# Biases of a linear attention carried by a constant feature of the normalised input, and the query feature map read from PSUM

## The chip, the cores and the metric

One core of one Trainium2 chip. The metric is the device time in microseconds (us) of one execution of the program. The engines are named as in the profile: PE is TensorE (matmul), PEld its weight load, DVE is VectorE, ACT is ScalarE, POOL is GpSimd, SP is SyncE, and a trailing q (SPq) is an engine's queue.

## The reference, cut to what matters

Four residual layers run on an input of 4 batches x 2048 tokens x 256 features. Only the first, a linear attention, is touched by the change:

```python
x = inputs                                    # (4, 2048, 256)
z = (x - mean(x)) / sqrt(var(x) + 1e-5)       # layer norm over the 256 features, no gain
q = elu(z @ Wq + bq) + 1;  k = elu(z @ Wk + bk) + 1;  v = z @ Wv + bv
kv = einsum('bkhd,bkhm->bhdm', k, v)          # 16 heads of 16
out = einsum('bqhd,bhdm->bqhm', q, kv) / max(einsum('bqhd,bkhd->bqh', q, k), 1e-6)
x = x + out @ Wo + bo
```

Then follow a feed-forward layer, a second attention that only reaches 16 tokens of each batch, and the feed-forward layer again. A normalised row has mean zero, so its 256 features sum to zero, and feature 255 is minus the sum of the others.

## The kernel before, in words

The 8192 tokens are cut into 16 groups (n = 0 to 15) of 512 tokens, four groups to a batch; a group is four tiles of 128 tokens. **Pass 1** (to about 190 us) computes for each group the normalised input, keys and queries, and adds k^T z up over a batch in PSUM; **pass 2** computes the attention output and the rest. Every engine has its own instruction stream, in an order written out by hand, and waits on semaphores. The change touches pass 1 and the loads ahead of it.

For each group in pass 1 PE runs, in this order: `k_product` (L1078: for each tile one bf16 matmul of `ones_row` by `bias3`, which puts bk + 1 into PSUM, then six fp32r matmuls of 256 columns, hi and lo halves of input and weights) into PB; at a batch's first group `g_transposes` of the batch before; `q_product` (L1091: 12 fp32r matmuls of 512 columns) into PA, with `kv_product` of the batch before in its middle at a batch's first group; `t1` (L1055: 8 transposes of the next group's normalised input into PT); `g_product` (L1105: 8 fp32 matmuls, 16 in the trace, of 257 columns: 256 features and a column of ones whose product is the sum of k) into PG.

ACT: normalises the next group (`ln1`, L516, four instructions at L513), takes exp of k - 1 (L541), then for each half of the queries exp (L548) and relu (L549), both with bq as bias, then copies the transposed input as `xt_hi` (`t1`, L524). DVE: `k_tok` = max(min(exp, 1), PSUM) (L722), statistics of the group after the next (L668, L671), at a batch's first group `batch_kv` (L740), `xt_lo` (L681), then the query step (L732), min(exp, 1) + relu, with both inputs in SBUF. Ahead of a batch's first group it copies PG to `g_sb` (`copy_g`, L734). PE's `q_product` waits on `q_relu` of the group before.

POOL turns statistics into scale and shift (`rstd`, L419, L424 to L430), and adds `bo` to x (`add_bo`, L441). POOL waits for `w2_loaded` (all seven start-up loads of L327 to L330) between its group 0 and its group 1:

```python
            ln1(0)
            pool.wait_ge(w2_loaded, 16 * 7)
            with pool.Fori(1, NG) as n:
                ln1(n)
                add_bo(n - 1)
```

The loads are issued by SP in the order x of group 0, Wq, Wk (L320), bk to three rows (L321), bq to a column (L323), Wr (L324), x of groups 1 to 3 (L326), then Wv, Wo, Ws1, Ws2, and bv, bo, ob, each spread to 128 rows (L330), then x of the groups from 4 on (L336). ACT waits for Wq and Wk (L527), splits both (L529), and only then normalises group 0. DVE computes the statistics of group 0, the lo halves (L689), the three-part bias (L693 to L700), the squares of Wr (L704) and `xt_lo` of group 0.

Of the kernel before, what the change touches and what calls it, by code (L numbers as in the profile page):

```python
# [13 lines left out]
P = 128  # L14
# [30 lines left out]
def hybrid_kernel(nc, x_in, Wq, bq, Wk, bk, Wv, bv, Wo, bo, qw, qb, kw, vw, vb, ow, ob,  # L45
# [11 lines left out]

    with ExitStack() as ctx:
# [53 lines left out]
        xn = [part(T * (D + 1)).rearrange("p (t d) -> p t d", t=T) for _ in range(2)]  # L112
# [7 lines left out]
        bias_rows = part(D)  # L120
        bpart = part(D).bitcast(BF16).rearrange("p (k n) -> p k n", k=2)
        used[0] = setup_start + 2 * C * GT
        wv, wo_raw = [part(C * D).rearrange("p (c n) -> p c n", c=C) for _ in range(2)]
        bv_rows, bo_rows = part(D), part(D)
        kv_tmp = part(C * P).rearrange("p (c n) -> p c n", c=C)
        g_sb = part(C * (D + 1)).rearrange("p (c n) -> p c n", c=C)
# [42 lines left out]
        def chunked(ap):  # L169
# [32 lines left out]
        w_loaded = sem("w_loaded")  # L202
        w2_loaded = sem("w2_loaded")
        wr_loaded = sem("wr_loaded")
        bias_loaded, bq_loaded = sem("bias_loaded"), sem("bq_loaded")
# [4 lines left out]
        bias_ready = sem("bias_ready")  # L210
# [106 lines left out]
        def _(sp):  # L317
            sp.dma_start(x_all[:, 0:T, :], x_dram[0]).then_inc(x_loaded[0], 16)
            for dst, w in ((wq_raw, Wq), (wk_raw, Wk)):
                sp.dma_start(dst, rows(w)).then_inc(w_loaded, 16)  # L320
            sp.dma_start(bias_rows[0:3, :], row(bk).to_broadcast([3, D])).then_inc(bias_loaded, 16)  # L321
            with nc.allow_non_contiguous_dma(reason="a short bias vector, features on partitions"):
                sp.dma_start(bq_col[:, :], bq.rearrange("(c p) -> p c", p=P)).then_inc(bq_loaded, 16)  # L323
# [74 lines left out]
        def _(pool):  # L398
# [47 lines left out]
            pool.wait_ge(w2_loaded, 16 * 7)  # L446
# [208 lines left out]
        def _(dve):  # L655
# [35 lines left out]
            dve.wait_ge(bias_loaded, 16)  # L691
            dve.wait_ge(consts, 5)
            link(nc.vector.tensor_scalar(bias_rows[0:3, :], bias_rows[0:3, :], 1.0, None, ALU.add))  # L693
            link(nc.vector.tensor_copy(bpart[0:3, 0, :], bias_rows[0:3, :]))
            link(nc.vector.tensor_tensor(bias_rows[0:3, :], bias_rows[0:3, :], bpart[0:3, 0, :], ALU.subtract))
            link(nc.vector.tensor_copy(bpart[0:3, 1, :], bias_rows[0:3, :]))
            link(nc.vector.tensor_tensor(bias_rows[0:3, :], bias_rows[0:3, :], bpart[0:3, 1, :], ALU.subtract))
            link(nc.vector.tensor_scalar(bias_rows[0:3, :], bias_rows[0:3, :], ident[0:3, 2:3], None, ALU.mult))
# [749 lines left out]
```

## Time and profile before

| | us |
|---|---|
| runs of the kernel before (three) | 505.45, 504.20, 504.93 |
| median | 504.93 |
| span of the profiled execution | 503.0 |
| PE / DVE / ACT / POOL busy | 454.9 / 332.7 / 271.8 / 191.4 |
| DMA moved in the profiled execution | 20.55 MB |

The span runs from the first to the last instruction of the profiled execution; the device time of that execution is not listed by itself. The median of the three runs lies 1.9 us above the span, which is what starting and ending the program adds around it. Pass 1 takes the first 190 us of the span, pass 2 the rest.

### The profile page before, as it was taken

The numbers are of one execution on the slowest core, as the hardware profiler recorded it, in microseconds if no ns is written. First come the engines' busy times: TensorE is split into PE (matmuls) and PEld (weight loads), VectorE is DVE, ScalarE is ACT, GpSimd is POOL, SyncE is SP. The second block draws the span as 40 slices with busy tenths as digits, with TensorE's granted clock in tenths as the row PEclk, the third lists the DMA queues.
The fourth block names the chain that finished last, engine by engine and source line by source line (L and its number), as shares of the span: only waits on it lengthen the run. The fifth ranks groups of instructions, "written<-read, shape, count | busy, mean of one in ns | idle before, by whom it ended". The sixth has DMA issues, their size and how long they took to land.

```text
span 503.0 us, 8738 instructions
## 1 busy us (share of the span) xinstructions
PE 454.9 (90%) x2737; PEld 369.5 (73%) x2737; DVE 332.7 (66%) x791; ACT 271.8 (54%) x465; POOL 191.4 (38%) x270
## 2 busy tenths in 40 slices
PE   1899999999999998779999899899999999996763
PEld 1888888888888887568787687576778776783441
DVE  4467766775775626365777867787876977786462
ACT  3466656665665552436566446455565465755330
POOL 2344333343433600433545436464442653334300
PEclk9999999999999999789999999999999999999895
DMA  8312111111000002000111011011101110111110
GB/s 265 122 53 76 42 43 42 44 55 43 27 1 1 1 15 70 1 1 2 61 43 51 2 44 44 1 45 43 43 3 44 44 42 1 42 42 44 41 45 7
DMA packets 22732, 20.55 MB, mean 41 GB/s; under 512 B 3155, under 2 KB 22678, under 8 KB 22678
## 3 DMA queue, kind: packets, MB, share of 16 engines
q1 hardware_dynamic: 22678, 19.92, 12.3%
q8 instruction: 23, 0.38, 0.3%
q14 instruction: 31, 0.25, 0.2%
HBM read 11.40 MB, written 8.45 MB: 39 GB/s over the span
## 4 chain that ended last, share of the span: by engine, by line
PE 61%; DVE 15%; issue 8%; ACT 6%; POOL 4%; SPq 2%; DMA 1%; DVEq 1%; POOLq 0%; ACTq 0%
PE PG L1110 8%; PE PA L1191 6%; PE PA L1211 4%; PE PG L1196 4%; PE PT L1183 3%; ACT scratch L513 3%; PE PB L1196 3%; DVE ln_bn L668 3%; PE PA L1102 3%; PE PA L1100 3%; PE PA L1101 3%; PE PB L1086 2%; PE PB L1088 2%; PE PB L1087 2%; PE PT L1061 2%
## 5 line engine op out<-in xcount | busy, mean ns | idle before, releaser
L513 ACT ACTIVATE scratch<-x_all,ln_shift,ln_rstd 128x256 f32<-128x256 f32 (+1 forms) x192 | 99.6, 589 | 69.1 <-POOL ln_shift L430 36.7
L424 POOL TENSOR_SCALAR ln_rstd<-ln_mv 128x4 f32<-128x4 f32 x48 | 10.8, 226 | 219.4 <-DVE ln_mv L671 210.0
L668 DVE BATCH_NORM_STATS2 ln_bn<-x_all 128x6 f32<-128x256 f32 (+1 forms) x192 | 67.2, 413 | 5.0 <-DMA x_all<-n_L_attn_a_inputs_q_dram 3.3
L1191 PE MATMUL PA<-scratch,ws 128*128 128x512 f32 x128 | 61.6, 604 | 1.5 <-ACT scratch L613 1.2
L1110 PE MATMUL PG<-scratch 128*128 128x257 f32 x256 | 58.5, 381 | 0.8 <-DVE scratch L722 0.8
L437 POOL TENSOR_TENSOR x_all<-x_all,ob_rows 128x1024 f32<-128x1024 f32 x16 | 37.9, 2369 | 40.3 <-ACT scratch L513 40.3
L1110 PEld LDWEIGHTS PG<-scratch 128*128 128x128 f32 x256 | 47.4, 190 | 7.7 <-issue 1.0
L426 POOL TENSOR_TENSOR ln_rstd<-ln_rstd,minus_half 128x4 f32<-128x4 f32 x48 | 49.8, 1038 | 4.0
L1183 PE MATMUL PT<-ident,scratch 128*128 128x128 f32 x256 | 36.6, 289 | 10.3 <-ACT scratch L513 9.2
L722 DVE SCALAR_TENSOR_TENSOR scratch<-scratch,PB 128x1024 f32<-128x1024 f32 x16 | 19.5, 1221 | 39.1 <-ACT scratch L541 39.1
L732 DVE SCALAR_TENSOR_TENSOR q_all<-scratch,q_all 128x1024 f32<-128x1024 f32 (+1 forms) x16 | 43.5, 2719 | 2.5 <-ACT q_all L549 2.5
L1086 PE MATMUL PB<-wk_hi,xt_hi 128*128 128x256 f32 x128 | 42.4, 331 | 0.0
L1183 PEld LDWEIGHTS PT<-ident,scratch 128*128 128x128 f32 x256 | 29.4, 147 | 16.1 <-ACT scratch L513 11.6
L437 POOL TENSOR_TENSOR x_all<-x_all,scratch 128x1024 f32 (+1 forms) x16 | 38.5, 2406 | 0.6 <-ACT scratch L513 0.6
L1191 PEld LDWEIGHTS PA<-scratch,ws 128*128 128x128 f32 x128 | 23.5, 195 | 18.6 <-issue 17.0
L1088 PE MATMUL PB<-wk_hi,xt_lo 128*128 128x256 f32 x128 | 36.8, 288 | 0.0
L1087 PE MATMUL PB<-wk_lo,xt_hi 128*128 128x256 f32 x128 | 36.7, 287 | 0.0
L681 DVE TENSOR_TENSOR xt_lo<-PT,xt_hi 128x512 fp32r<-128x512 f32 x32 | 20.7, 686 | 22.8 <-ACT xt_hi L524 22.7
L1248 PE MATMUL PB<-wo_hi,o_hi 128*128 128x256 f32 x128 | 34.0, 299 | 1.0 <-ACT o_hi L599 0.8
L852 DVE TENSOR_TENSOR x_all<-PB,x_all 128x1024 f32<-128x1024 f32 (+1 forms) x16 | 19.5, 1220 | 22.8 <-PE PB L1254 21.0
L548 ACT ACTIVATE scratch<-PA,bq_col 128x512 f32<-128x512 f32 x32 | 22.0, 688 | 22.4 <-DVE scratch L722 19.2
L594 ACT ACTIVATE scratch<-PT 128x512 f32<-128x512 f32 x32 | 17.6, 595 | 29.0 <-PE PT L1183 29.0
(194 smaller groups left out, 1029.0 us busy)
## 6 DMA issues: line engine op xcount, KB each, us to landing
x_all<-n_L_attn_a_inputs_q_dram SPq DMA_DIRECT2D x16, 512.0 KB, 3.6
out_dram<-scratch SPq DMA_DIRECT2D x16, 512.0 KB, 2.8
scratch<-in_L_attn_a_Wq_dram SPq DMA_DIRECT2D x1, 256.0 KB, 3.7
scratch<-in_L_attn_a_Wk_dram SPq DMA_DIRECT2D x1, 256.0 KB, 5.5
scratch<-in_L_attn_a_Wv_dram SPq DMA_DIRECT2D x1, 256.0 KB, 6.7
scratch<-in_L_attn_a_Wo_dram SPq DMA_DIRECT2D x1, 256.0 KB, 5.3
ws<-in_L_ffn_Ws_dram SPq DMA_DIRECT2D x2, 128.0 KB, 5.2
b_weights<-in_L_attn_b_qw_dram SPq DMA_DIRECT2D x1, 256.0 KB, 2.7
```

Of the source, the lines that this page charges most:

```text
L426: nc.gpsimd.tensor_tensor(ln_rstd[:, slot, :], ln_rstd[:, slot, :], minus_half[:, 0:T], ALU.pow).then_inc(powed, 1)
L437: nc.gpsimd.tensor_tensor(x_group(n), x_group(n), rows_[:, :].rearrange("p (o d) -> p o d", o=1).to_broadcast([P, T, D]), ALU.add).then_in ...
L513: nc.scalar.activation(dst[:, t:t + 1, 0:D], x_tile(n, t), ACT.Identity, scale=ln_rstd[:, slot, t:t + 1], bias=ln_shift[:, slot, t:t + 1]) ...
L668: nc.vector.bn_stats(ln_bn[:, slot, t:t + 1, :], x_tile(n, t)).then_inc(bn, 1)
L732: nc.vector.scalar_tensor_tensor(q, exp_q, 1.0, q, ALU.min, ALU.add).then_inc(q_done, 1)
L1086: mm(dst, hi, wk_hi[:, c, :], start=False, stop=False)
L1087: mm(dst, hi, wk_lo[:, c, :], start=False, stop=False)
L1088: last = mm(dst, lo, wk_hi[:, c, :], start=False, stop=(c == C - 1))
L1110: last = mm(PG[:, c, 0:D + 1], k_tok[:, t, c * P:(c + 1) * P], xn[g % 2][:, t, :], start=(g == 0 and t == 0), stop=(g == G - 1 and t == T ...
L1183: last = nc.tensor.transpose(dst[:, c, t * P:(t + 1) * P], src[:, t, c * P:(c + 1) * P], ident[:, :])
L1191: last = mm(dst, ws1[:, c, :], xt[:, c, :], start=(c == 0), stop=(c == C - 1))
L1196: last = mm(four(pair)[:, t, :], h[:, t * P:(t + 1) * P], ws2[:, :], start=True, stop=True)
```

## The change

Feature 255 of the normalised input is no longer computed: POOL sets that column of both buffers to 1 once, and ACT writes features 0 to 254. The weights are loaded with rows 0 to 254 in place and the bias as row 255; DVE then subtracts the old last row from the rows 0 to 254 and, for Wk and Wq, adds 1 to the bias row. So the matmuls give k + bk + 1 and q + bq + 1 with no bias matmul. The sum of k is now column 255 of `g_product`, so its 257th column goes. For the queries ACT takes exp(q - 1) in one instruction of 1024 columns and DVE computes max(min(exp, 1), PSUM) as for the keys, and PE waits for that DVE step. The loads of Wq move from SP's queue to ACT's.

```diff
+    def load_with_bias(eng, dst, last_row, w, b, loaded):
+        eng.dma_start(dst[:, 0, :], w[0:P, :]).then_inc(loaded, 16)
+        eng.dma_start(dst[0:P - 1, 1, :], w[P:D - 1, :]).then_inc(loaded, 16)
+        eng.dma_start(dst[P - 1:P, 1, :], row(b)).then_inc(loaded, 16)
+        eng.dma_start(last_row, w[D - 1:D, :].to_broadcast([P, D])).then_inc(loaded, 16)
...
 SP
             sp.dma_start(x_all[:, 0:T, :], x_dram[0]).then_inc(x_loaded[0], 16)
-            for dst, w in ((wq_raw, Wq), (wk_raw, Wk)):
-                sp.dma_start(dst, rows(w)).then_inc(w_loaded, 16)
-            sp.dma_start(bias_rows[0:3, :], row(bk).to_broadcast([3, D])).then_inc(bias_loaded, 16)
-                sp.dma_start(bq_col[:, :], bq.rearrange("(c p) -> p c", p=P)).then_inc(bq_loaded, 16)
+            load_with_bias(sp, wk_raw, wk_last, Wk, bk, w_loaded)
             sp.dma_start(wr[:, :, :], rows(Wr)).then_inc(wr_loaded, 16)
             for g in range(1, G):
                 sp.dma_start(x_all[:, g * T:(g + 1) * T, :], x_dram[g]).then_inc(x_loaded[g], 16)
-            for dst, w in ((wv, rows(Wv)), (wo_raw, rows(Wo)),
-                           (ws1[:, :, :], rows(Ws1)), (ws2[:, :], Ws2), (bv_rows[:, :], row(bv).to_broadcast([P, D])),
+            load_with_bias(sp, wv, wv_last, Wv, bv, w2_loaded)
+            for dst, w in ((wo_raw, rows(Wo)), (ws1[:, :, :], rows(Ws1)), (ws2[:, :], Ws2),
                            (bo_rows[:, :], ...), (ob_rows[:, :], ...)):
                 sp.dma_start(dst, w).then_inc(w2_loaded, 16)
 POOL
-            nc.gpsimd.memset(ones_row[:, :], 1.0).then_inc(consts, 1)
-                nc.gpsimd.memset(xn[i][:, :, D:D + 1], 1.0).then_inc(consts, 1)
+                nc.gpsimd.memset(xn[i][:, :, D - 1:D], 1.0).then_inc(consts, 1)
...
-            pool.wait_ge(w2_loaded, 16 * 7)
+            pool.wait_ge(w2_loaded, 16 * 9)
 ACT
-            act.wait_ge(w_loaded, 32)
-            for hi, raw in ((wq_hi, wq_raw), (wk_hi, wk_raw)):
-                nc.scalar.activation(hi[:, :, :], raw, ACT.Copy).then_inc(w_split, 1)
+            load_with_bias(act, wq_raw, wq_last, Wq, bq, wq_loaded)
+            act.wait_ge(wk_row, 3)
+            nc.scalar.activation(wk_hi[:, :, :], wk_raw, ACT.Copy).then_inc(w_split, 1)
             ln1(0, 0)
+            act.wait_ge(wq_row, 3)
+            nc.scalar.activation(wq_hi[:, :, :], wq_raw, ACT.Copy).then_inc(w_split, 1)
...
-                    for c in range(C):
-                        ge_apart(act, "act", q_mm, C * n + c + 1)
-                        nc.scalar.activation(exp_q[:, c, :], PA[:, c, :], ACT.Exp, bias=bq_col[:, c:c + 1]).then_inc(q_exp, 1)
-                        nc.scalar.activation(q_all[:, bass.ds(n * C + c, 1), :], PA[:, c:c + 1, :], ACT.Relu,
-                                             bias=bq_col[:, c:c + 1]).then_inc(q_relu, 1)
+                    ge_apart(act, "act", q_mm, C * (n + 1))
+                    nc.scalar.activation(exp_q, PA[:, :, :], ACT.Exp, bias=minus_one[:, 0:1]).then_inc(q_exp, 1)
 DVE
+            def take_last_row(w, last_row, done, one):
+                nc.vector.tensor_tensor(w[:, 0, :], w[:, 0, :], last_row, ALU.subtract).then_inc(done, 1)
+                nc.vector.scalar_tensor_tensor(w[:, 1, :], last_row, but_last[:, 0:1], w[:, 1, :], ALU.mult, ALU.add).then_inc(done, 1)
+                if one:
+                    dve.wait_ge(done, 2)
+                    nc.vector.tensor_scalar(w[:, 1, :], w[:, 1, :], ident[:, P - 1:P], None, ALU.add).then_inc(done, 1)
             ln1(0, 0, 0)
+            dve.wait_ge(w_loaded, 16 * 4)
+            take_last_row(wk_raw, wk_last, wk_row, True)
+            dve.wait_ge(wq_loaded, 16 * 4)
+            take_last_row(wq_raw, wq_last, wq_row, True)
...
-            (L691 to L701: the eight instructions of the three-part bias)
...
-                    ge_apart(dve, "dve", q_relu, C * (n + 1))
-                    q = q_all[:, bass.ds(n * C, C), :]
-                    nc.vector.scalar_tensor_tensor(q, exp_q, 1.0, q, ALU.min, ALU.add).then_inc(q_done, 1)
+                    ge_apart(dve, "dve", q_exp, n + 1)
+                    nc.vector.scalar_tensor_tensor(q_all[:, bass.ds(n * C, C), :], exp_q, 1.0, PA[:, :, :],
+                                                   ALU.min, ALU.max).then_inc(q_done, 1)
...
                 for c in range(C):
-                    nc.vector.scalar_tensor_tensor(kv_tmp[:, c, :], bv_rows[...], g_sb[:, c, D:D + 1], PG[:, c, D:D + P], ...)
...
             pass1(0, False)
+            dve.wait_ge(w2_loaded, 16 * 9)
+            take_last_row(wv, wv_last, wv_row, False)
 PE
-                    mm(dst, ones_row[:, :], bias3[:, :], start=True, stop=False)
...
-                ge(pe, q_relu, C * n)
+                ge(pe, q_done, n)
...
-                        last = mm(PG[:, c, 0:D + 1], k_tok[:, t, c * P:(c + 1) * P], xn[g % 2][:, t, :],
+                        last = mm(PG[:, c, 0:D], k_tok[:, t, c * P:(c + 1) * P], xn[g % 2][:, t, :],
...
+                pe.wait_ge(wv_row, 2)          (in kv_product)
```

## Rows read from the trace of the kernel before

**Rows 1.** Stretch: length, busy us of PE, PEld, DVE, ACT, POOL; clock, DMA share, GB/s.

```profile
105.00:147.00 42.00, 41.92 (x256) 36.73 (x255) 28.10 (x56) 25.88 (x44) 14.58 (x21) 1.00 0.08 25
```

**Rows 2.** PE in time order, group 2: start us, us, engine, line, operation.

```profile
38.48 0.27 PE L1083 MATMUL PB<-bias,ones_row 128*128 128x256 bf16 x1
...
39.31 0.28 PE L1083 MATMUL PB<-bias,ones_row 128*128 128x256 bf16 x1
...
45.46 3.64 PE L1110 MATMUL PG<-scratch 128*128 128x257 f32 x16
48.93 0.27 PE L1083 MATMUL PB<-bias,ones_row 128*128 128x256 bf16 x1
```

**Rows 3.** PE in time order, four places with idle time (in brackets, with its releaser).

```profile
14.03 0.37 PE L1083 MATMUL PB<-bias,ones_row 128*128 128x256 bf16 x1 [0.48 <-DVE xt_lo L681]
...
23.78 3.71 PE L1110 MATMUL PG<-scratch 128*128 128x257 f32 x16 [0.82 <-DVE scratch L722]
28.03 0.28 PE L1083 MATMUL PB<-bias,ones_row 128*128 128x256 bf16 x1 [0.53 <-DVE xt_lo L681]
...
63.51 0.66 PE L1118 MATMUL PG<-ident,scratch 128*128 128x128 f32 x4 [0.61 <-DVE scratch L738]
```

**Rows 4.** Who waited for whom at the weight load: total us, times, longest.

```profile
PEld PG L1118 <- DVE scratch L738: 1.4, 3, 0.8
```

**Rows 5.** DVE in time order, group 3.

```profile
53.64 1.22 DVE L722 SCALAR_TENSOR_TENSOR scratch<-scratch,PB 128x1024 f32<-128x1024 f32 x1 [1.85 <-ACT scratch L541]
...
59.11 3.14 DVE L732 SCALAR_TENSOR_TENSOR q_all<-scratch,q_all 128x1024 f32<-128x1024 f32 x1
62.17 0.68 DVE L758 TENSOR_TENSOR wo_lo<-scratch,wo_hi 128x512 fp32r<-128x512 f32 x1
```

**Rows 6.** ACT in time order, group 3.

```profile
52.49 1.12 ACT L541 ACTIVATE scratch<-PB,minus_one 128x1024 f32<-128x1024 f32 x1 [1.27 <-PE PB L1088]
54.90 0.69 ACT L548 ACTIVATE scratch<-PA,bq_col 128x512 f32<-128x512 f32 x1 [1.29 <-DVE scratch L722]
...
57.19 1.10 ACT L524 ACTIVATE xt_hi<-PT 128x512 fp32r<-128x512 f32 x2
```

**Rows 7.** The chain that ended last, its part at the start: start us, us, what.

```profile
10.20 6.48 DMA ob_rows<-in_L_attn_b_ob_dram
17.14 0.21 POOL ln_rstd L424
...
19.30 1.48 ACT scratch L513 x3
...
22.42 1.23 DVE scratch L722
```

**Rows 8.** Start-up load L321 (bk, spread to three rows).

```profile
L321 SPq DMA_DIRECT2D scratch<-in_L_attn_a_bk_dram x1: 396/396/396, 2.4 to 2.4; - x1
```

**Rows 9.** Its neighbour, start-up load L323 (bq, to 128 rows).

```profile
L323 SPq DMA_DIRECT2D bq_col<-in_L_attn_a_bq_dram x1: 382/382/382, 2.8 to 2.8; - x1
...
DMA to landing us min/median/max: 4.7/4.7/4.7
```

**Rows 10.** Two stretches of the start, columns as in rows 1.

```profile
0.00:2.50 2.50, 0.00 (x0) 0.00 (x0) 0.22 (x2) 1.28 (x1) 1.61 (x13) 1.00 0.13 17
7.50:12.50 5.00, 1.91 (x8) 1.57 (x8) 4.26 (x12) 3.54 (x7) 0.47 (x3) 1.00 1.08 361
```

**Rows 11.** Lines of DVE in the first 14 us: busy us, mean ns.

```profile
L699 DVE SCALAR_TENSOR_TENSOR scratch<-scratch,ident 3x256 f32<-3x256 bf16 x1 | 0.5, 473 | 0.0
...
L695 DVE TENSOR_TENSOR scratch<-scratch 3x256 f32<-3x256 f32 x1 | 0.4, 411 | 0.0
```

**Rows 12.** ACT in time order at the start: group 0 is normalised.

```profile
8.39 2.06 ACT L513 ACTIVATE scratch<-x_all,ln_shift,ln_rstd 128x256 f32<-128x256 f32 x4
```

**Rows 13.** Two stretches of pass 2, columns as in rows 1: PE idle, then at work.

```profile
219.80:222.90 3.10, 0.00 (x0) 0.00 (x0) 3.03 (x10) 1.63 (x4) 1.21 (x3) 1.00 0.00 0
222.90:226.30 3.40, 2.90 (x14) 2.91 (x15) 1.17 (x7) 1.64 (x3) 2.71 (x3) 0.50 0.00 0
```

More of the change, by code:

```diff
@@ L110, in part @@
             return a
-        xn = [part(T * (D + 1)).rearrange("p (t d) -> p t d", t=T) for _ in range(2)]
+        xn = [part(T * D).rearrange("p (t d) -> p t d", t=T) for _ in range(2)]
         k_tok = part(T * D).rearrange("p (t d) -> p t d", t=T)
@@ L119, in hybrid_kernel @@
         wk_raw = part(C * D).rearrange("p (c n) -> p c n", c=C)
-        bias_rows = part(D)
-        bpart = part(D).bitcast(BF16).rearrange("p (k n) -> p k n", k=2)
+        wq_last, wk_last = part(D), part(D)
         used[0] = setup_start + 2 * C * GT
         wv, wo_raw = [part(C * D).rearrange("p (c n) -> p c n", c=C) for _ in range(2)]
-        bv_rows, bo_rows = part(D), part(D)
-        kv_tmp = part(C * P).rearrange("p (c n) -> p c n", c=C)
-        g_sb = part(C * (D + 1)).rearrange("p (c n) -> p c n", c=C)
+        wv_last, bo_rows = part(D), part(D)
+        g_sb = part(C * D).rearrange("p (c n) -> p c n", c=C)
         used[0] = 0
@@ L199, in hybrid_kernel @@
         h_s = last_q[1](SP)
-        w_loaded = sem("w_loaded")
+        w_loaded, wq_loaded = sem("w_loaded"), sem("wq_loaded")
         w2_loaded = sem("w2_loaded")
         wr_loaded = sem("wr_loaded")
-        bias_loaded, bq_loaded = sem("bias_loaded"), sem("bq_loaded")
         consts = sem("consts")
@@ L508, in _, with normalise @@
         def _(act):
-            def normalise(dst, n, slot, j, ready, done):
+            def normalise(dst, n, slot, j, ready, done, width=D):
                 ge_apart(act, "act", ready, j + 1)
                 for t in range(T):
-                    nc.scalar.activation(dst[:, t:t + 1, 0:D], x_tile(n, t), ACT.Identity, scale=ln_rstd[:, slot, t:t + 1],
+                    nc.scalar.activation(dst[:, t:t + 1, 0:width], x_tile(n, t)[:, :, 0:width], ACT.Identity, scale=ln_rstd[:, slot, t:t + 1],
                                          bias=ln_shift[:, slot, t:t + 1]).then_inc(done, 1)
@@ L517, in ln1 @@
                 ge_apart(act, "act", g_mm, n - 1)
-                normalise(xn[g % 2], n, 0, n, rstd1, norm1)
+                normalise(xn[g % 2], n, 0, n, rstd1, norm1, D - 1)
             def t1(n, g):
@@ L559, in _ @@
             act.wait_ge(setup_dve, 1)
-            act.wait_ge(bq_loaded, 16)
             pass1(0, False)
-            act.wait_ge(w2_loaded, 16 * 7)
+            act.wait_ge(w2_loaded, 16 * 9)
             nc.scalar.activation(wo_hi[:, :, :], wo_raw, ACT.Copy).then_inc(w_split, 1)
@@ L688, in _ @@
+            ln1(0, 0, 0)
+            dve.wait_ge(setup_dve, 2)
+            dve.wait_ge(w_loaded, 16 * 4)
+            take_last_row(wk_raw, wk_last, wk_row, True)
+            dve.wait_ge(wq_loaded, 16 * 4)
+            take_last_row(wq_raw, wq_last, wq_row, True)
+            for i, (lo, hi, raw) in enumerate(((wk_lo, wk_hi, wk_raw), (wq_lo, wq_hi, wq_raw))):
                 dve.wait_ge(w_split, i + 1)
                 nc.vector.tensor_tensor(lo[:, :, :], raw, hi[:, :, :].bitcast(F32), ALU.subtract).then_inc(setup_dve, 1)
-            dve.wait_ge(bias_loaded, 16)
@@ L692, in _ @@
[L692 to L697, printed above, removed]
@@ L743, in batch_kv @@
                 for c in range(C):
-                    nc.vector.scalar_tensor_tensor(kv_tmp[:, c, :], bv_rows[:, c * P:(c + 1) * P], g_sb[:, c, D:D + 1],
-                                                   PG[:, c, D:D + P], ALU.mult, ALU.add).then_inc(kv_step, 1)
-                for c in range(C):
-                    dve.wait_ge(kv_step, C * b + c + 1)
                     dst = kv_all[:, bass.ds(b * C + c, 1), :]
                     nc.vector.tensor_tensor(dst[:, :, 0:P].rearrange("p o (h e) -> p (o h) e", e=HD),
-                                            kv_tmp[:, c, :].rearrange("p (h e) -> p h e", e=HD),
+                                            PG[:, c, D:D + P].rearrange("p (h e) -> p h e", e=HD),
                                             head_mask[:, :].rearrange("p (h o) -> p h o", o=1).to_broadcast([P, HC, HD]),
```

33 lines of the change are left out of this document (13 added, 20 removed).

## The prediction

> **What bounds the kernel now.** I read the busy time by stretch first: in 42 us of the middle of pass 1, PE is busy 41.92 us at a granted clock of 1.00, which is its higher level, 2.4 GHz; DVE has 28.1 and ACT 25.9 [rows 1]. So pass 1 costs what PE issues. The time order of PE says how much that is for one group: `k_product` of group 2 starts at 38.48, that of group 3 at 48.93, 10.45 us with no idle row between [rows 2]. The waits of PE then show where pass 1 is not PE's alone: at the start, and at the first group of each later batch [rows 3, 4]. The chain that ended last tells which wait rules the start. It is not PE's work but the last start-up load: `ob_rows` is issued at 10.20 and lands at 16.68, POOL starts group 1's scale at 17.14, ACT normalises group 1 from 19.30, takes exp of k from 21.4, DVE forms `k_tok` from 22.42, and PE begins `g_product` of group 0 at 23.78 after 0.82 us idle [rows 3, 7]. Whatever PE saves before 23.78 is lost in that wait; whatever the loads lose is paid in full.
>
> **The gain, part by part.** *Bias matmuls.* A tile's seven matmuls take 39.31 - 38.48 = 0.83 us, 0.12 each [rows 2]; one of seven goes. Four per group give 0.48 us, and 15 groups behind the start 7.2 us; group 0's share is lost in the wait. *257th column.* `g_product` takes 48.93 - 45.46 = 3.47 us for 257 columns [rows 2]; a 257th of it, 15 times, is 0.2 us. *Query step.* Four instructions of ACT, 57.19 - 54.90 = 2.29 us up to the copy `xt_hi`, become one like L541, 1.12 us [rows 6], and DVE's 3.14 us become 1.22 us, as L722 with one input in PSUM [rows 5]. In a PE-bound group that gives nothing: it hides under `g_product`. Where PE waited for `xt_lo`, at 28.03, it removes 0.53 us [rows 3]. `g_transposes` waited for `copy_g`, which is queued on DVE behind the query step, three times, 1.4 us at the weight load, 0.61 of it plainly idle PE at 63.51 [rows 3, 4]. With DVE 1.9 us earlier two of these go. At the first the new `take_last_row` of Wv (0.41 + 0.47 us [rows 11]) and `wo_lo` (0.68) stand ahead of the copy, so about 0.2 us stays. With the shorter `batch_kv` (two instructions of six less) I take 1.1 us, between 0.6 and 1.6.
>
> *New waits.* PE's `q_product` now waits for DVE's query step of the group before. That step ends 1.2 us after `xt_lo`, which itself releases `k_product`, 2.87 us long: cost nothing; even at the old 3.14 us it would end about when `q_product` starts, since `xt_lo` comes 1.1 us sooner. ACT's exp waits for both halves, but ends no later after the second than exp and relu of that half did. Gain: 7.2 + 0.2 + 0.53 + 1.1 = **9.0 us** (8 to 9.6).
>
> **The loads.** They carry the forecast. Each weight is loaded in four pieces, and the second has 127 rows, once for Wk and Wv on SP's queue and once for Wq on ACT's. How many DMA engines share such a load the trace does not show directly. What it shows: the load of three rows is the only start-up load for which the view of a line gives no landing, while its neighbour to 128 rows has one [rows 8, 9]; a full landing is sixteen engines reporting, so the three rows were not dealt over sixteen. Equal shares by row is the simplest rule that fits both, and 127 is prime: one engine. The bounds of a 127-row piece: 8 rows on the fullest engine (even deal) or 127 on one. I take the second. A row costs one engine 1 KB at 361/16 = 22.6 GB/s, that is 45 ns [rows 10]: 0.4 or 5.7 us. I also take the same engine for all three pieces, the first, since a deal without memory begins there each time; the other reading is a rival below. The Trainium skill ("DMA: Bandwidth & Descriptors", section "Why a DMA increments its semaphore by 16 and not by 1") says that the count of engines is the largest number up to 16 that divides the outermost dimensions, and that it is always the lowest-numbered ones. By that all three pieces, and every one-row load, share the same engine; no row here shows the choice of engine.
>
> Rows on that engine, at 1/16 of every 128-row load: on SP's queue x 32, Wk 8 + 127, bk 1, last row of Wk 8, together **176** up to `w_loaded`; on ACT's queue Wq 8 + 127 + 1 + 8 = **144**; then SP's Wr (32-byte rows, 3 in cost), three x 96, Wv 144, Wo 16, Ws1 and Ws2 18, bo and ob 16, together 293. If the two queues alternate, `wq_loaded` comes at 288 rows and `w_loaded` at 320, the last load at 613. The data start at about 2.5 us [rows 10]:
> - `w_loaded`: 2.5 + 320 x 0.045 = 16.9 us. DVE fixes Wk in 1.2 us (0.41, 0.47 and one more with a wait [rows 11]), ACT splits it in 0.6, then normalises group 0 in 2.06 [rows 12], from about 18.7. It did so from 8.39, and `k_product` started at 14.03 [rows 3, 12]; 10.3 us later is 24.3. Queued behind DVE's waits are the squares of Wr, `xt_lo` and group 1's statistics; PE has `k_product` and `q_product` done by about 31.7 (5.1 + 2.75 us before, less 0.5 of bias).
> - `w2_loaded`: 2.5 + 613 x 0.045 = 30.1 us against 16.68 [rows 7], **13.4 us** later. POOL, ACT, DVE follow as before, so `g_product` of group 0 starts at 23.78 + 13.4 = 37.2. This is the later of the two paths.
>
> ACT issues its four loads and SP two more than before, about 0.4 us each [rows 8]: hidden under the transfers. The eight instructions of the three-part bias on DVE, and POOL's memsets, go for nothing, since DVE then waits for loads anyway. PE would sit idle some 3 us before 35. After a stretch of 3.1 us without a matmul the trace has 3.4 us at a clock of 0.50, the 1.2 GHz level [rows 13]. Here most of such a stretch would pass in waiting; 0 to 1.7 us, I take 0.8. Pass 2 is not touched: the last query step starts well inside the last `g_product`.
>
> Sum: 13.4 + 0.8 - 9.0 = **+5.2 us**, span 503.0 to 508.2. The median of the runs is 1.9 us above the span, so 504.93 + 5.2 = **510.1 us**.
>
> **Rivals.** *Even deal (0.13).* The 127 rows are dealt 8 to an engine. The start then moves by the extra bytes: two loads of 128 KB more, 0.7 us at 361 GB/s, less the 256 four-byte rows of bq, and `x` of group 0 shares the engines with Wq: -0.5 to 1.5, I take 0.4. 504.93 - 9.0 + 0.4 = **496.3 us**, clearly faster. For it: nothing in the trace has 127 rows. Against: the three-row load. *One engine each, but three different ones (0.15).* The fullest has 613 - 3 x 127 = 232 rows plus 127: 2.5 + 359 x 0.045 = 18.7, 2.0 us late; `w_loaded` waits for 193 rows, 11.2 us, so `k_product` at 18.7, and PE reaches `g_product` 0 at 27.0, 3.2 us late. 504.93 - 9.0 + 3.2 = **499.1 us**. It decides for faster as long as `g_product` 0 starts less than 9 us later than 23.78; above that point the forecast holds. *Query step does not shrink (within the above).* If DVE stays at 3.14 us, only about 0.7 us of the gain goes.
>
> **How the numbers follow.** The forecast has 0.72: equal shares is the simplest reading, but its evidence is one missing landing. Its own range: 43 to 46 ns a row, up to 2 us of stalls in a queue that everything passes through, clock 0 to 1.7, gain 8 to 9.6, so 506 to 514.5. With 0.28 on the faster cases the range must reach one of them: 498 to 514.5 leaves out the even deal and some tails. A measurement of this kernel can tell about 0.3%, 1.5 us, from no change. Slower: 0.72 less what of it lies below 506.4, 0.68; same 0.06; faster 0.13 + 0.13 = 0.26.
>
> **What would show it.** Right: bias matmuls gone, k pitch of a tile 0.71 us, group period 10.45 to 9.95, DVE's query step 1.22 us; DMA share falling to about 0.06 with GB/s near 23 from some 12 us on, while loads are still open; POOL's first wait on the last load ending near 30 us and `g_product` 0 near 37; ACT's first normalise near 18.7. Wrong: the last load landing before 20 us (even deal or several engines), or a group period that stays above 10.2 because some step of ACT or DVE, hidden now, ends after `g_product`.

## The result and the profile after

The kernel after took 513.06 us in the median of four runs (512.03 to 514.03), beside 504.71 us (504.20 to 505.45) for the kernel before in the same series: 8.35 us more, a ratio of 1.0173 with a 95% interval of 1.0132 to 1.0214. A later series on one chip gave 513.02 against 505.22 us, 1.0156 (1.0132 to 1.0179). The forecast was slower, 510.1 us, in a range of 498.0 to 514.5. The profiled execution took 512.03 us, with a span of 510.3 against 503.0.

The busy time by stretch, kernel after; columns as in [rows 1].

```profile
105.00:147.00 42.00, 42.00 (x258) 37.87 (x256) 23.29 (x54) 21.62 (x33) 17.17 (x23) 1.00 0.15 49
...
3.00:4.50 1.50, 0.00 (x0) 0.00 (x0) 0.00 (x0) 0.00 (x0) 0.00 (x0) 1.00 1.04 367
...
8.50:9.50 1.00, 0.00 (x0) 0.00 (x0) 0.00 (x0) 0.00 (x0) 0.33 (x2) 1.00 0.07 23
...
35.60:42.40 6.80, 6.29 (x18) 5.10 (x19) 5.23 (x12) 3.17 (x5) 2.50 (x6) 0.50 0.19 63
```

The first row answers to [rows 1]: the middle of pass 1 is still PE's alone, and DVE and ACT have 4 to 5 us less to do in 42 us. The second and third row are the loads: at 3 us all engines together move 367 GB/s, at 9 us 23 GB/s, which is one sixteenth of it, at a share of 0.07, where the kernel before has 361 GB/s [rows 10]. The last row is PE at a granted clock of 0.50, the 1.2 GHz level.

The DMA queues in the third of these stretches, 8.50 to 9.50: q1 is SP's queue, and q10, which the kernel before without loads on ACT does not have, is ACT's; packets, MB, share of 16 engines' time.

```profile
q10 hardware_dynamic: 11, 0.01, 3.5%
q1 hardware_dynamic: 11, 0.01, 3.4%
```

Each queue moves 11 packets of 1 KB in this microsecond, and both together take 6.9% of the engines' time, about one sixteenth (6.25%): the two queues share one engine. From 5 to 6 us, with SP's queue all but still, ACT's alone moves 22 packets. That is 45 ns a row, as forecast.

PE in time order, kernel after: start us, us, then the idle time before it with its releaser.

```profile
25.31 0.55 PE L1080 MATMUL PB<-wk_hi,xt_hi 128*128 128x256 f32 x1 [0.85 <-DVE xt_lo L676]
...
35.73 1.97 PE L1057 MATMUL PT<-ident,scratch 128*128 128x128 f32 x8 [3.04 <-ACT scratch L510]
38.08 5.85 PE L1104 MATMUL PG<-scratch 128*128 128x256 f32 x16 [0.38 <-DVE scratch L720]
43.57 0.47 PE L1080 MATMUL PB<-wk_hi,xt_hi 128*128 128x256 f32 x1
...
53.53 0.47 PE L1080 MATMUL PB<-wk_hi,xt_hi 128*128 128x256 f32 x1
...
63.47 0.47 PE L1080 MATMUL PB<-wk_hi,xt_hi 128*128 128x256 f32 x1
...
77.36 0.66 PE L1112 MATMUL PG<-ident,scratch 128*128 128x128 f32 x4 [0.73 <-DVE scratch L736]
...
193.90 3.62 PE L1104 MATMUL PG<-scratch 128*128 128x256 f32 x16
```

`g_product` of group 0 starts at 38.08 where it started at 23.78 [rows 3], 14.30 us later. From then on PE has no idle row until 77.36, and a group takes 63.47 - 53.53 = 9.94 us in place of 10.45 [rows 2]. The last `g_product` of pass 1 starts at 193.90, against 186.46 before: the start cost twice what the rest of pass 1 gave back.

The chain that ended last, kernel after, its part at the start: start us, us, what.

```profile
1.85 0.37 SPq L61
2.27 7.10 SPq L62
...
15.52 1.81 SPq L60
...
17.71 4.74 SPq L62
...
24.86 6.15 DMA ob_rows<-in_L_attn_b_ob_dram
31.75 1.04 POOL ln_rstd L423
...
36.71 1.23 DVE scratch L720
38.08 5.85 PE PG L1104 x16
```

L61 is the load of 127 rows, L62 the one-row load behind it. `ob_rows` is issued at 24.86 and lands at 24.86 + 6.15 = 31.01, 14.33 us later than the 16.68 of before; its own time to landing is the same 6 us [rows 7]. From the landing to `g_product` it is 7.07 us, before 7.10. So all of this delay lies ahead of the issue of the last load, and here is a row that the prediction did not have: SP stands in L62 for 7.10 us and again for 4.74 us, where an issue took 0.40 us before [rows 8].

DVE in time order, kernel after.

```profile
17.89 0.42 DVE L684 TENSOR_TENSOR scratch<-scratch 128x256 f32<-128x256 f32 x1 [11.03 <-DMA scratch<-in_L_attn_a_Wk_dram]
...
72.45 1.21 DVE L729 SCALAR_TENSOR_TENSOR q_all<-scratch,PA 128x1024 f32<-128x1024 f32 x1
73.58 2.13 DVE L684 TENSOR_TENSOR scratch<-scratch 128x256 f32<-128x256 f32 x1
```

The query step is 1.21 us, where it was 3.14 [rows 5]. But the same subtraction L684 that takes 0.42 us on Wk takes 2.13 us on Wv: behind it come L685, `wo_lo` and `copy_g`, which ends at 77.31, and this is what `g_transposes` waits for at 77.36.

### The profile page after: what moved, and what is told of

The parts are those of the page before. It is cut to its first block, busy times and chain, and to the rows that moved or that the text cites. A ratio compares the mean times of both kernels' runs of the same rounds, so it can differ in the third digit from the quotient of the medians.

```text
span 510.3 us, 8529 instructions
## 1 busy us (share of the span) xinstructions
PE 448.5 (88%) x2673; PEld 367.0 (72%) x2673; DVE 308.5 (60%) x783; ACT 250.6 (49%) x417; POOL 190.7 (37%) x269
## 4 chain that ended last, share of the span: by engine, by line
PE 63%; DVE 14%; issue 6%; ACT 5%; SPq 5%; POOL 4%; DMA 1%; DVEq 0%; POOLq 0%; ACTq 0%
PE PG L1104 11%; PE PA L1186 6%; PE PA L1206 4%; PE PG L1191 4%; PE PT L1178 3%; ACT scratch L510 3%; PE PB L1191 3%; DVE ln_bn L663 3%; PE PA L1094 3%; PE PA L1095 3%; PE PA L1096 3%; PE PB L1081 3%; PE PB L1082 3%; PE PB L1080 3%; SPq L62 2%
## 5 line engine op out<-in xcount | busy, mean ns | idle before, releaser
L510 ACT ACTIVATE scratch<-x_all,ln_shift,ln_rstd 128x256 f32<-128x256 f32 (+3 forms) x192 | 99.5, 589 | 84.8 <-POOL ln_shift L427 35.1
L1104 PE MATMUL PG<-scratch 128*128 128x256 f32 x256 | 60.1, 389 | 0.4 <-DVE scratch L720 0.4
L1104 PEld LDWEIGHTS PG<-scratch 128*128 128x128 f32 x256 | 48.9, 196 | 7.3 <-issue 0.7
L1178 PE MATMUL PT<-ident,scratch 128*128 128x128 f32 x256 | 36.6, 289 | 10.2 <-ACT scratch L510 9.2
L1178 PEld LDWEIGHTS PT<-ident,scratch 128*128 128x128 f32 x256 | 29.4, 147 | 16.0 <-ACT scratch L510 11.6
L1080 PE MATMUL PB<-wk_hi,xt_hi 128*128 128x256 f32 x128 | 39.8, 311 | 0.8 <-DVE xt_lo L676 0.8
L1057 PE MATMUL PT<-ident,scratch 128*128 128x128 f32 x128 | 18.4, 291 | 24.9 <-ACT scratch L510 24.9
L1057 PEld LDWEIGHTS PT<-ident,scratch 128*128 128x128 f32 x128 | 16.2, 151 | 27.1 <-issue 21.8
L546 ACT ACTIVATE scratch<-PA,minus_one 128x1024 f32<-128x1024 f32 x16 | 17.9, 1116 | 30.5 <-PE PA L1096 29.2
L1191 PE MATMUL PG<-ws,scratch 128*128 128x256 f32 x128 | 32.4, 397 | 0.4
```

What stands on the lines that cost most here:

```text
L510: nc.scalar.activation(dst[:, t:t + 1, 0:width], x_tile(n, t)[:, :, 0:width], ACT.Identity, scale=ln_rstd[:, slot, t:t + 1], bias=ln_shift ...
L1057: last = nc.tensor.transpose(PT[:, c, t * P:(t + 1) * P], xn[g % 2][:, t, c * P:(c + 1) * P], ident[:, :])
L1080: mm(dst, hi, wk_hi[:, c, :], start=(c == 0), stop=False)
L1104: last = mm(PG[:, c, 0:D], k_tok[:, t, c * P:(c + 1) * P], xn[g % 2][:, t, :], start=(g == 0 and t == 0), stop=(g == G - 1 and t == T - 1))
L1178: last = nc.tensor.transpose(dst[:, c, t * P:(t + 1) * P], src[:, t, c * P:(c + 1) * P], ident[:, :])
L1191: last = mm(four(pair)[:, t, :], h[:, t * P:(t + 1) * P], ws2[:, :], start=True, stop=True)
```

## The experiments

Where a time of the whole kernel is given, it is the median, and the kernel before of the same series stands beside it. "Last g" is the start of the last `g_product` of pass 1 in the profiled run (186.46 before, 193.90 after): it separates what pass 1 does from what pass 2 varies by.

### The 127 rows in two pieces

```diff
-        eng.dma_start(dst[0:P - 1, 1, :], w[P:D - 1, :]).then_inc(loaded, 16)
+        eng.dma_start(dst[0:P - 16, 1, :], w[P:D - 16, :]).then_inc(loaded, 16)
+        eng.dma_start(dst[P - 16:P - 1, 1, :], w[D - 16:D - 1, :]).then_inc(loaded, 16)
```

112 rows and 15 rows, the waits counted up to fit; all else is the kernel after.

> The kernel after, with each 127-row load issued as 112 + 15 rows; nothing left out. One-engine theory: 112 rows go 7 to an engine over 16, 15 rows one to an engine over 15, so nothing queues on one engine; the last start-up load lands near 17 to 18 us instead of 31.0, g_product of group 0 starts near 24 to 25 instead of 38.1, no stretch at half clock at the start, and the time is 504.7 - 9 + 0.4 to 1.5, about 496 to 497.5 us. Rival, the bytes or the two queues cost the time, not the 127 rows: the last landing stays near 30 us and the time near 513. Rival, the query step read from PSUM or its new wait cost something too: landing near 17, but the time stays above 500.

496.49 us (before: 506.35), 0.9807 (0.9778 to 0.9837). SP in time order, the kernel with 112 + 15 rows:

```profile
1.85 0.43 SPq L61 DMA_DIRECT2D scratch<-in_L_attn_a_Wk_dram  x1
2.33 0.49 SPq L62 DMA_DIRECT2D scratch<-in_L_attn_a_Wk_dram  x1
2.86 0.24 SPq L63 DMA_DIRECT2D scratch<-in_L_attn_a_bk_dram  x1
...
11.04 0.43 SPq L329 DMA_DIRECT2D ob_rows<-in_L_attn_b_ob_dram  x1
```

PE in time order, same kernel:

```profile
15.45 0.55 PE L1081 MATMUL PB<-wk_hi,xt_hi 128*128 128x256 f32 x1 [0.85 <-DVE xt_lo L677]
...
24.14 3.62 PE L1105 MATMUL PG<-scratch 128*128 128x256 f32 x16
...
61.21 0.66 PE L1113 MATMUL PG<-ident,scratch 128*128 128x128 f32 x4 [0.74 <-DVE scratch L737]
...
177.79 3.62 PE L1105 MATMUL PG<-scratch 128*128 128x256 f32 x16
```

No issue is held up any more: the one-row load takes 0.24 us, and the last load is issued at 11.04 in place of 24.86; no load is open any more from 17.0 on, and POOL starts group 1's scale at 17.17. `g_product` 0 starts at 24.14, the last one at 177.79, 16.1 us ahead of the kernel after. The whole loss of pass 1 sits in how the 127 rows are cut; everything else in the change is a gain of 8.7 us (186.46 - 177.79).

### The pieces put into the kernel before

```diff
+            def in_pieces(dst, w, loaded):
+                sp.dma_start(dst[:, 0, :], w[0:P, :]).then_inc(loaded, 16)
+                sp.dma_start(dst[0:P - 1, 1, :], w[P:D - 1, :]).then_inc(loaded, 16)
+                sp.dma_start(dst[P - 1:P, 1, :], w[D - 1:D, :]).then_inc(loaded, 16)
-            for dst, w in ((wq_raw, Wq), (wk_raw, Wk)):
-                sp.dma_start(dst, rows(w)).then_inc(w_loaded, 16)
+            in_pieces(wq_raw, Wq, w_loaded)
+            in_pieces(wk_raw, Wk, w_loaded)
```

and the same for Wv. The kernel before is otherwise untouched, and all three stay on SP's queue.

> The kernel before, with Wq, Wk and Wv each loaded as 128 + 127 + 1 rows on SP's queue; nothing else changed, nothing left out. One-engine theory: the fullest engine carries about 237 + 3 x 120 = 597 rows of 1 KB at 45 ns, so the last start-up load lands near 2.5 + 26.9 = 29.4 us instead of 16.7, and g_product of group 0 starts some 12.7 us later, part of it at half clock (0 to 2.4 us): 504.7 + 12.7 + 0 to 2.4 = 517 to 520 us. Rival, the loss of the kernel after needs its other parts (Wq on ACT's queue, the broadcast last rows, DVE's fixing of the weights): the time is within 3 us of 504.7.

521.01 us (before: 506.35), 1.0305 (1.0276 to 1.0335). POOL in time order:

```profile
31.07 0.23 POOL L430 TENSOR_SCALAR ln_rstd<-ln_mv 128x4 f32<-128x4 f32 x1 [23.03 <-DMA ob_rows<-in_L_attn_b_ob_dram]
```

PE in time order, same kernel:

```profile
37.73 4.25 PE L1116 MATMUL PG<-scratch 128*128 128x257 f32 x16 [0.38 <-DVE scratch L728]
...
200.44 3.64 PE L1116 MATMUL PG<-scratch 128*128 128x257 f32 x16
```

The cut alone, with no gain beside it, costs 200.44 - 186.46 = 14.0 us in pass 1. The time of 521.01 beside 506.35 is 1.0305 of it, 520.1 us on the scale of 504.7: the upper end of what was expected. POOL, released by the last load, starts within 0.4 us of the kernel after (31.07 here, 31.44 there), though here all three pieces are on one queue and there one of them is on ACT's. If the queue chose the engine, moving Wq to ACT's queue would have taken 127 rows off it. It did not. SP in time order, same kernel, has the first one-row load of this kernel:

```profile
2.23 3.51 SPq L322 DMA_DIRECT2D scratch<-in_L_attn_a_Wq_dram  x1
```

It holds SP for 3.51 us with nothing on ACT's queue, and for 7.10 us in the kernel after with ACT's piece beside it: the second queue's rows go through the same engine.

### One piece of 127 rows instead of three

```diff
-            load_with_bias(sp, wv, wv_last, Wv, bv, w2_loaded)
+            load_with_bias(sp, wv, wv_last, Wv, bv, w2_loaded, whole=True)
```

In the kernel with 112 + 15 rows Wv alone is loaded with its 127 rows in one.

> e1_split with one of the three second pieces, that of Wv, again as one load of 127 rows; nothing left out. One-engine theory: the fullest engine carries 613 - 2 x 119 = 375 rows, 2.5 + 16.9 = 19.4 us and up to 1 us of stalls, so POOL starts group 1's scale near 19.8 to 20.8 instead of 17.2 and the time is 2.5 to 3.7 us above e1_split. Rival, the three loads each cost their own fixed time in the queue, a third of the 13 us each: 4 us or more above e1_split. Rival, it is the wait for Wk and Wq alone: no more than 0.5 us above.

502.57 us (before: 504.92), 0.9951 (0.9926 to 0.9976). PE in time order:

```profile
25.67 1.97 PE L1061 MATMUL PT<-ident,scratch 128*128 128x128 f32 x8 [3.08 <-ACT scratch L514]
28.02 5.84 PE L1108 MATMUL PG<-scratch 128*128 128x256 f32 x16 [0.38 <-DVE scratch L724]
33.50 0.47 PE L1084 MATMUL PB<-wk_hi,xt_hi 128*128 128x256 f32 x1
...
183.87 3.62 PE L1108 MATMUL PG<-scratch 128*128 128x256 f32 x16
```

`g_product` 0 is 3.9 us late (28.02 against 24.14), and the last one 6.1 us (183.87 against 177.79). The 2.2 us between the two are the clock: after 3.08 us idle `g_product` 0 takes 33.50 - 28.02 = 5.48 us. The last load is issued at 15.04 and lands 5.92 us later, at 20.96, and POOL starts at 21.38 where 19.8 to 20.8 was expected: the landing is 1.6 us later than the 19.4 of the row sum, and the clock was left out. By the medians the kernel takes 0.9951 of the time before against 0.9807 to 0.9821 with 112 + 15 rows, some 7 us more where 2.5 to 3.7 was expected. The number alone would fit the first rival, a fixed time for each load: one piece moves the landing by 4.3 us from the 16.68 of the kernel before, two more by another 10.05 us (20.96 to 31.01). What speaks for rows on one engine is the rate of 23 GB/s and the packets that the two queues deal out in turn, not this run.

### The kernel after with PE kept at work

```diff
+                    if isinstance(n, int) and n == 0:
+                        pe.wait_ge(flag_ready, 1)
+                        for _ in range(7):
+                            mm(PG[:, 1, 0:D], ones_f[:, :], ws_fill, start=True, stop=True)
```

Seven matmuls, 14 in the trace, whose product nobody reads, between `q_product` and `t1` of group 0.

> The kernel after, with seven fp32 matmuls of 256 columns (3.0 us at full clock) put into the time in which PE waits between q_product of group 0 and the transposes of group 1; their product is overwritten, nothing left out. If the idle 3.04 us is what sets the clock to half from 35.6 to 42.4: g_product of group 0 runs in 3.5 instead of 5.5 us, the clock stays at 1.00, and the time falls by 1.5 to 2.1 us to about 511.3. Rival, the half clock does not come from this idle stretch: the row of g_product keeps its 5.5 us and the time stays at 513.1 or rises.

511.89 us (before: 506.35), 1.0099 (1.0061 to 1.0137). PE in time order:

```profile
32.40 3.19 PE L1138 MATMUL PG<-scratch,ones_f 128*128 128x256 f32 x14
...
37.97 3.69 PE L1104 MATMUL PG<-scratch 128*128 128x256 f32 x16 [1.25 <-DVE scratch L720]
41.31 0.47 PE L1080 MATMUL PB<-wk_hi,xt_hi 128*128 128x256 f32 x1
...
191.67 3.62 PE L1104 MATMUL PG<-scratch 128*128 128x256 f32 x16
```

The same stretch as in the kernel after, by stretches:

```profile
35.60:42.40 6.80, 5.53 (x32) 4.91 (x33) 5.23 (x12) 3.61 (x6) 2.50 (x6) 1.00 0.24 77
```

`g_product` 0 starts where it did (37.97 against 38.08), but at a clock of 1.00: 3.34 us to the next `k_product` where the kernel after has 5.49. The idle PE costs 2.15 us on top of the late load, and the last g is 2.23 us earlier. By the medians, 1.0099 (1.0061 to 1.0137) against 1.0156 (1.0132 to 1.0179), the two kernels are hardly told apart, so the reading rests on these rows. The spans of the two profiled runs are equal all the same, 510.3 us: this run has a stretch of half clock in pass 2, at 325.5, which the kernel after lacks.

### The bias matmul alone

```diff
-                    mm(dst, ones_row[:, :], bias3[:, :], start=True, stop=False)
```

In the kernel before; the first matmul of a tile then starts the sum. The keys are computed without bk + 1.

> The kernel before without the bias matmul of k_product: k is computed without bk + 1, everything else runs. If a bias matmul costs 0.12 us of PE in 15 of 16 groups: group period 10.45 to 9.97, time 504.7 - 7.2 - up to 0.5 = 497 to 497.5 us, and the wait of k_product of group 1 for xt_lo and those of g_transposes for copy_g stay or grow a little, since the query step is the old one. Rival, with PE faster the old query step of DVE and ACT becomes the bound: the period stays above 10.2 and the time above 501.

497.62 us (before: 506.35), 0.9844 (0.9810 to 0.9878). Last g at 179.54, 6.9 us earlier; 0.5 us of it is there at `g_product` 0 (23.28 against 23.78), since POOL was released sooner in this profiled run (16.39 against 17.12). Waits of PE from 20 to 200 us: total us, times, longest.

```profile
PE PG L1117 <- DVE scratch L738: 2.2, 3, 1.1
...
PE PB L1085 <- DVE xt_lo L681: 0.4, 1, 0.4
```

The waits of `g_transposes` for `copy_g` grow from 0.6 us to 2.2, since PE arrives earlier and DVE does not: PE now sits idle at all three batch starts, for 1.1 us at the longest, where it did at one [rows 3].

### The old query step in the kernel with 112 + 15 rows

```diff
-                    nc.scalar.activation(exp_q, PA[:, :, :], ACT.Exp, bias=minus_one[:, 0:1]).then_inc(q_exp, 1)
+                    for c in range(C):
+                        nc.scalar.activation(exp_q[:, c, :], PA[:, c, :], ACT.Exp, ...).then_inc(q_exp, 1)
+                        nc.scalar.activation(q_all[...], PA[:, c:c + 1, :], ACT.Relu, ...).then_inc(q_relu, 1)
```

and DVE's min and add on two inputs in SBUF, with PE waiting on `q_relu`, as before.

> e1_split with the query step as before: ACT takes exp and relu of each half (bias -1), DVE adds them from SBUF, PE waits for relu; nothing left out. If the new query step is worth what the kernel without the bias matmul suggests (0.4 us at the first k_product behind a query step, 0.5 to 0.9 us at each of three batch starts), the time is 1.5 to 2.5 us above e1_split, near 497 us on the scale where the kernel before has 504.7, with the group period still 9.95 us inside a batch. Rival, the query step is hidden everywhere: within 0.5 us of e1_split. Rival, PE waits in every group: the period rises above 10.1 and the time by over 3 us.

501.43 us (before: 504.92), 0.9929 (0.9905 to 0.9954). Waits of PE from 20 to 200 us, the kernel with the old query step:

```profile
PE PG L1116 <- DVE scratch L740: 3.0, 3, 1.9
...
PE PG L1108 <- DVE scratch L724: 0.7, 1, 0.7
...
PE PB L1084 <- DVE xt_lo L680: 0.5, 1, 0.5
```

DVE in time order, same kernel, at the first batch's end:

```profile
57.84 3.15 DVE L734 SCALAR_TENSOR_TENSOR q_all<-scratch,q_all 128x1024 f32<-128x1024 f32 x1
60.92 0.41 DVE L688 TENSOR_TENSOR scratch<-scratch 128x256 f32<-128x256 f32 x1
```

The query step takes 3.15 us again, while the subtraction behind it (L688 here, L684 in the kernel after) takes 0.41 us instead of 2.13. POOL's addition of `bo` ran from 57.52 to 59.91 and was over by then.

Last g at 181.24, 3.45 us behind 177.79, where 1.5 to 2.5 was expected. The wait for `copy_g` is 3.0 us in three places, 0.7 in the kernel with the new step: 2.3 us. From `g_product` 0 to the next `k_product` it is 28.15 - 23.91 = 4.24 us instead of 27.41 - 24.14 = 3.27, 1.0 us, 0.5 of it the wait for `xt_lo`. The 0.7 us that `g_product` 0 waits costs nothing, since it starts 0.2 us sooner than with the new step. Inside a batch the groups take 9.93 to 9.96 us in the first batch and 9.96 to 10.19 later, so the rival in which PE waits in every group holds in the time and not in its mechanism. By the medians the step is worth more, 0.9929 against 0.9821 or 1.1%; the spans of the profiled runs differ by 3.5 to 4.2 us (499.7 against 496.2 and 495.5), and the rest was not taken apart.

### A version that should beat both

To the kernel with 112 + 15 rows: `bo` is loaded early on a semaphore of its own, and POOL waits for it alone; DVE takes the statistics of group 1 ahead of the lo halves; ACT normalises group 0 ahead of `wk_hi`; the old last row of Wv is taken off behind the query step of group 1.

```diff
-            pool.wait_ge(w2_loaded, 16 * 10)
+            pool.wait_ge(bo_loaded, 16)
...
+                    if isinstance(n, int) and n == 1:
+                        dve.wait_ge(w2_loaded, 16 * 9)
+                        take_last_row(wv, wv_last, wv_row, False)
```

> e1_split with four moves, nothing left out: POOL waits for a bo of its own, loaded early, instead of for all loads; DVE does group 1's statistics ahead of the lo halves; ACT normalises group 0 before it splits Wk; DVE fixes Wv behind group 1's query step instead of at the batch's end, where it held up copy_g. Expected: k_product of group 0 starts 0.4 us sooner, g_product of group 0 behind PE's own work at about 23.3 instead of 24.1, and the 0.7 us wait at the first g_transposes goes: 1.2 to 1.8 us below e1_split, about 493.5 us on the scale of 504.7. Rival, the start is not on the path any more or the Wv step holds up another group: no gain.

495.97 us (before: 504.92), 0.9822 (0.9785 to 0.9858). A variant with Wq on SP's queue:

> best1 with the five loads of Wq on SP's queue behind those of Wk, instead of on ACT's; nothing left out. If Wq on a second queue delays x of group 0 (its statistics start at 5.45 us in e1_split, at 4.39 in the kernel before), they start near 4.4 again and k_product of group 0 up to 0.9 us sooner: up to 0.9 us below best1. Rival, the later x of group 1 or Wq itself then sets the start: same as best1 or up to 1 us above.

498.13 us, 0.9868 (0.9828 to 0.9909): `x` of group 0 comes an us sooner, `x` of group 1 later, and `k_product` 0 starts at 16.89 in place of 14.92, so it is the rival that came. Then the kernels with and without the four edits, and the kernel after, on one chip:

> The kernel of e1_split once more, beside the next two on one chip, since pass 2 gains or loses single 3.4 us stretches at half clock from run to run and the comparison with best1 spans two chips so far. One-engine theory: 8 to 10 us below the kernel before and 15 to 19 us below the kernel after.

> The kernel of best1 once more. Its last g_product starts 1.6 us before that of e1_split in the two profiles; if that reaches the end, it lies 1 to 2 us below e1_again. Rival: the half-clock stretches of pass 2 take it back, and the two cannot be told apart.

> The kernel after, once more, beside e1_again: 7 to 10 us above the kernel before.

With 505.22 us for the kernel before: 496.47 (0.9795 to 0.9846) for 112 + 15 rows alone, 496.89 (0.9815 to 0.9864) with the four edits, 513.02 for the kernel after. In the trace the edits do their work, PE in time order in the kernel with all four:

```profile
14.92 0.55 PE L1084 MATMUL PB<-wk_hi,xt_hi 128*128 128x256 f32 x1 [0.58 <-DVE xt_lo L679]
...
23.31 3.62 PE L1108 MATMUL PG<-scratch 128*128 128x256 f32 x16
...
176.21 3.62 PE L1108 MATMUL PG<-scratch 128*128 128x256 f32 x16
```

1.6 us in pass 1, and no idle PE at the batch's start, but 495.97 and 496.89 us where 493.5 was expected: over the whole kernel this is within what runs differ by. The version to keep is the plain one: the change with 127 cut into 112 + 15, 8.8 us below the kernel before and 16.6 below the change as it was made.

## Why the prediction was right, and where its sizes were off

**Sign and mechanism: right.** The last start-up load rules the start, it became late because 127 rows go through one DMA engine, and PE's gain behind it is smaller. The kernel with 112 + 15 rows shows it from one side, the kernel before with the pieces from the other: +14.0 us in pass 1 from the cut alone.

**One engine, and the same for all pieces: right.** The evidence was one missing landing in [rows 8]. The stretch at 9 us now shows it directly: 23 GB/s is 367/16. That SP's and ACT's pieces share the engine is there in the same microsecond, 11 packets for each queue, and the kernel before with all three on SP's queue, whose last load lands at 30.65 against 31.01, agrees. The rival with three different engines had `k_product` 0 at 18.7 and `g_product` 0 at 27.0; the trace has 25.31 and 38.08. The even deal had 496.3 us, 8.6 less than before; 112 + 15 rows measure 496.5, 8.75 less than the kernel before beside it in the later series and 9.9 less in the first. That is as it should be: this cut spreads the load, and it tests the rest of the sum by itself.

The rule that the prediction cited from the Trainium skill ("DMA: Bandwidth & Descriptors", section "Why a DMA increments its semaphore by 16 and not by 1") names 127 partitions as a case of one engine and has the lowest-numbered engine for each. These runs agree as far as they reach: the 127 rows go at one engine's rate, and both queues' pieces take the same engine; which one it is, no row shows.

**Rows and landing: 0.9 us short, and in part by luck.** 2.5 + 613 x 0.045 = 30.1 was forecast, 31.0 measured; `w_loaded` was to come at 16.9, DVE starts on Wk at 17.89; the first normalise was to start at 18.7, ACT starts it at 19.67. The 13.4 us set a landing by formula against a measured one. By the same formula the kernel before, with some 237 rows on its fullest engine, lands at 2.5 + 237 x 0.045 = 13.2 us, and it landed at 16.68. The kernels with one piece (375 rows, 19.4) and with the pieces in the kernel before (597 rows, 29.4) landed at 20.96 and 30.65. So the formula is early everywhere, and the less so the more rows there are; formula against formula would have been 16.9 us, and 14.33 was measured. Two pieces more, 238 rows, cost 10.05 us, 42 ns a row: that part of the term holds. What makes the rest later is open. The 361 GB/s do not hold throughout (the kernel before moves 125 GB/s from 14 to 15 us), and no run tested why.

The sentence "ACT issues its four loads and SP two more than before, about 0.4 us each: hidden" is wrong in its size. The one-row load took 7.10 us to issue on SP, 4.74 the second time, 3.23 on ACT, and SP issued nothing in between. It is hardly what made `w_loaded` 1.0 us late: the last load that it counts was issued at 9.41, some 8 us before, and from 10 to 15 us ACT's queue went on at 10 to 12 packets a microsecond, its half of the engine, so up to there the engine did not run dry. Behind that it did shape the path: the last load could be issued only at 24.86, and from 25.50 to 31.00 all engines were at work again, at 299 GB/s. So the row sum has the size of the delay, but not the picture of one engine at work by itself up to the end. A kernel whose queue carried something urgent behind would have paid the 7 us.

**The clock: 0.8 us taken, 2.15 measured.** "Here most of such a stretch would pass in waiting; 0 to 1.7 us, I take 0.8" is the term that was mis-sized, and its upper end was too low. [rows 13] gave a stretch of 3.4 us at half clock, but here it lasted 6.8 us, from 35.6 on, with PE's transposes and nearly all of `g_product` in it. The clock fell after 3.04 us idle, as forecast. The price was read from the kernel with PE kept at work: 5.49 - 3.34 us. It is no fixed price: in the kernel before with the pieces, 3.28 us of idle PE were followed by half clock from 35.39 to 38.60 only, and from `g_product` 0 to the next `k_product` it was 4.25 us, as in the kernel before.

**The gain: 9.0 us taken.** From `g_product` 0 to the last one it took 186.46 - 23.78 = 162.68 us before and 177.79 - 24.14 = 153.65 with 112 + 15 rows: 9.03 us. The sum was right, its parts less so, and that they add up to it is luck. The bias matmuls and the column: 15 groups at 10.45 - 9.94 = 0.51 us are 7.65 us (forecast 7.4). The query step, of which "only about 0.7 us of the gain goes" if DVE stays at 3.14 us, is worth 3.45 us: once PE's group is half a us shorter, DVE's old 3.14 us is what `copy_g` stands behind, 3.0 us of waits in place of 0.6. The two parts of the gain cover each other: the bias matmul alone gives 6.4 us from `g_product` 0 on, where 7.2 was forecast, and its absence makes the query step dear. At the first batch's start, where 0.2 us was to stay, 0.7 stays: L684 took 2.13 us and not 0.41.

**The sum again, with what was measured.** Landing and start of `g_product` 0 +14.30 (forecast 13.4), half clock +2.15 (0.8), and from there to the last `g_product` -9.03 (-9.0): +7.4, and 193.90 - 186.46 = 7.44. Forecast was +5.2. The spans of the two profiled runs differ by 7.3 us and the medians by 8.35; the rest is not in pass 1 and is no more than what runs of one kernel differ by.

**The chances.** 0.72 on the right case, with a range to 514.5 that held 513.06 by little. Its upper end had 1.7 us for the clock where 2.15 was due, and its lower end of 506 does not follow from the terms given: with 43 ns a row, the whole gain of 9.6 and no clock they make 507.5.

## What to carry to other kernels

Look at the number of rows of each load, and do not leave it at 127: here 127 rows as 112 + 15 turn a loss of 8 us into a gain of 9. Watch for one semaphore that gathers all start-up loads while only one of them is needed (POOL needed `bo`): whatever slows any of them lands on the path. And cost a saving on one engine again at the period that the other saving leaves: a step that was hidden under PE was not hidden once PE was 5% faster.

## What the runs showed of the hardware

- **The issue of a load can be held up by rows issued before it.** L62, a load of one row, held SP for 7.10 us behind the 127 rows of Wk, and for 4.74 us behind those of Wv; on ACT's queue it was 3.23 us. With the 127 rows cut in two the same one-row load took 0.24 us. That it waits for room on the one engine is the likely reading; no row shows what it waits for.
- **DVE with both inputs in SBUF waits for POOL.** L684 took 0.42 us twice and 2.13 us the third time. POOL in time order, kernel after:

```profile
73.04 2.39 POOL L434 TENSOR_TENSOR x_all<-x_all,scratch 128x1024 f32 x1
```

  DVE's L684 starts at 73.58 and ends at 75.71; POOL's addition of `bo` runs from 73.04 to about 75.4. The kernel before has the same in its query step. Of the 16, the eleven that start 0.2 to 0.4 us behind the start of an addition take 3.14 to 3.22 us, the three that start later in one take 1.77 to 2.31, and the two that meet none take 1.21 and 1.23. DVE in time order, kernel before:

```profile
180.08 1.21 DVE L732 SCALAR_TENSOR_TENSOR q_all<-scratch,q_all 128x1024 f32<-128x1024 f32 x1
```

  So the 3.14 us of [rows 5] was no price of the operation. With one input in PSUM it was 1.21 or 1.22 us in all 16 groups, also where an addition ran beside it (84.65 in the kernel after, with POOL at it from 83.02 to 85.38). The Trainium skill ("SBUF — State Buffer", section "SBUF: two separate sides") has one pair of ports that DVE, with two inputs in SBUF, and a GpSimd instruction that reads SBUF take in turn for a whole instruction; these rows agree.
- **Half clock is paid by what comes after.** 3.04 and 3.08 us without a matmul were followed by 5.49 and 5.48 us for a `g_product` that takes 3.34. In pass 2 single stretches of this kind stand in one profiled run and not in another: one at 325.5 with PE kept at work, and the equal spans say that pass 2 took back the 2.2 us of pass 1. That is enough to hide gains as small as that of the last version.
